# A four-layer graph network on one core: attention sum, norm and last table pass in one stage, weighing on VectorE, and one TensorE signal per four steps

## The chip, the cores and the metric

The kernel runs on one core of one Trainium2 chip. The metric is the device time in microseconds (us). The kernel before took 8360.5 us, the median of three runs (8353.5 to 8371.33).

## What is computed

A graph with 6250 nodes of 256 features and 100000 edges, sorted by target node, goes through four layers. Each is a residual sum followed by a layer norm:

```python
x = _layernorm(x + _L0_gnn_ref(x, src, dst, edge_type_32, edge_weight1, ...))   # 32 relations
x = _layernorm(x + _L1_gnn_ref(x, edge_weight1, ..., src, dst, edge_type_16))   # 16 relations, gated
x = _layernorm(x + _L2_gnn_ref(x, W, a_src, a_dst, edge_W, edge_b, bias, ...))  # attention, 8 heads
x = _layernorm(x + _L3_gnn_ref(x, weight, edge_weight1, src, dst, edge_type_20))# 20 relations
```

Layers 0, 1 and 3 are relational: every node is multiplied with a 256x256 matrix per relation (a table of node x relation rows), each edge takes the row of its source and its relation times its weight, the rows are summed by target, then relu. Layer 2 is attention: for each edge and head a score, a softmax over the edges of one target, and

```python
attn = ex / jnp.maximum(denom[dst], 1e-10)
out = jax.ops.segment_sum(h_src * attn[..., None], dst, num_segments=n)
return out.reshape(n, H * D) + bias
```

## The kernel before

Nodes are held in windows of 128 (NW1 = 49 windows with nodes, NWIN = 50 with one of padding). The edges are cut into 782 tiles of 128; a tile that crosses into another window is visited once per window, so there are STEPS = 830 steps, rounded up to KP = 832. SLOT = 17 steps stand for one window. One **step** sums one tile: a 128x128 matrix of marks (which edge belongs to which row of the window) is the moving or stationary operand of one f32 matmul on TensorE (PE) with the tile's 128 rows, and VectorE (DVE) adds the result in PSUM to the window's rows. The trace shows such an f32 matmul as two records.

The program is a list of stages with a barrier between them (`run`, `PHASES`). In time order: setup and weights; three table passes of layer 0; "fused" (first walk, its norm and the table of layer 1); "gat" (second walk, norm and the attention projections); scores; softmax; "gather_sum"; "norm"; two table passes of layer 3; and "last" (third walk, norm, output).

**A walk** ("fused", "gat", "last") is written out step by step, without a hardware loop. GpSimd (POOL) gathers the rows of step s out of the table with one indirect DMA (L574) into a ring of NR = 16 slots, after waiting for `step_done` of step s - 16. PE's `step` waits for the marks, for the gather of its slot and for the addition that frees its PSUM bank (three banks in "fused", SB1 = 4 in the other two), then multiplies (L1297) and signals `step_done` after each step. DVE, in `fused_steps`, reads the window's number from `win` (L752), waits for `step_done`, makes the mark of step s + 8 (L788), and adds (L806). Between its steps it does parts of the previous window's norm (`row_norm`, L766 to L776, and `normalise_row`).

**The attention sum** ("gather_sum") is a hardware loop. SP loads eight tiles of saved rows at a time (`reload`, L528, 128x8x264 values), ACT copies the softmax numerators into their first eight columns (`exps`, L1226), POOL multiplies eight tiles in one instruction (`weigh`, L596), DVE builds marks (L732) and adds 264 columns (L747), PE multiplies (L1456).

**Norm** (`residual_norm`, L909 to L932) divides, adds the residual and takes mean and variance over all windows at once. **The passes** of layer 3 (`Pass`, 10 relations each) split the weights in a high and a low part, transpose each window, and for each of the 50 windows and 5 PSUM banks run six 128x512 matmuls (L1280); ACT empties each bank (L1129), SP stores it to the table (L387). They are hardware loops too. "fused" does the same for layer 1 inside its walk: eight banks per window (L1321) between the steps.

Quoted from the walk's DVE part, since all turns on its order:

```python
dve.wait_ge(wk.step_done, s + 1)
if s + G < KP:
    mark(s + G)
if s:
    dve.wait_ge(wk.added, s)
a = acc_[:, bass.ds(window, 1), :].squeeze(1)
dve.tensor_tensor(a, a, ps[:, s % banks, 0:D], ALU.add).then_inc(wk.added, 1)
```

## Time and profile before

| | |
|---|---|
| median of 3 runs | 8360.5 us (8353.5 to 8371.33) |
| the profiled execution, its own time | 8366.55 us |
| its span (first to last instruction) | 8364.7 us |
| PE, PE weight loads, DVE, ACT, POOL busy | 68%, 49%, 45%, 20%, 43% |
| granted TensorE clock, mean | 0.802 |
| moved by DMA | 1231.38 MB, 147 GB/s |

Read the shares with care: they are means over stages that have different limits. The page's forty slices show it at once (each digit is the busy share of a slice of 209 us in tenths):

```
PE   5999996888886555555555555555266665999555554
DVE  2111113555554555544444445687776111444444
```

so what a stage costs, and what waits last in it, is read from that stage alone.

### The profile page before, as it was taken

What the parts mean: (1) busy time and instruction counts of PE and PEld (TensorE: products, weight loads), DVE (VectorE), ACT (ScalarE), POOL (GpSimd) and SP (SyncE); (2) the same over time, 40 slices, a digit from 0 to 9 for tenths busy, and PEclk for the clock granted to TensorE, in tenths of its full rate; (3) what the DMA queues carried; (4) which work ended last, traced back from release to release, by engine and by line L of the source; (5) the groups of instructions that cost most, each with busy time, mean ns of one, the idle gap of its engine ahead of it and who ended that gap; (6) DMA issues with size and microseconds to landing.
All of it is one profiled execution on the core that took longest, in us unless ns stands there. A gap on an engine that the chain in (4) does not pass through costs nothing. (4 is left out here: it accounts for less than half of the span.)

```text
span 8364.7 us, 88481 instructions
## 1 busy us (share of the span) xinstructions
PE 5697.3 (68%) x20891; PEld 4066.0 (49%) x20892; DVE 3801.3 (45%) x9956; ACT 1686.8 (20%) x3167; POOL 3568.4 (43%) x3450
## 2 busy tenths in 40 slices
PE   5999996888886555555555555266665999555554
PEld 2878785666665333333333333134443878333333
DVE  2111113555554555544444445687776111444444
ACT  1444442333332000001111111100001444000000
POOL 0000003666665666665555555044341000566665
PEclk8999998999998767676676677577777999766666
DMA  5444444555554333334555556033332444333333
GB/s 163 187 186 186 172 188 158 185 186 187 186 181 145 109 107 108 108 109 145 189 186 189 189 187 199 34 117 122 114 124 105 186 172 186 115 98 95 98 96 94
DMA packets 395622, 1231.38 MB, mean 147 GB/s; under 512 B 101090, under 2 KB 169420, under 8 KB 355141
## 3 DMA queue, kind: packets, MB, share of 16 engines
q1 hardware_dynamic: 234645, 784.90, 25.1%
q0 software_dynamic: 160752, 443.96, 18.5%
q8 instruction: 82, 1.34, 0.1%
q14 instruction: 143, 1.17, 0.0%
HBM read 636.14 MB, written 592.41 MB: 147 GB/s over the span
## 5 line engine op out<-in xcount | busy, mean ns | idle before, releaser
L574 POOL DMA_INDIRECT ring<-table,idx x2496 | 2373.1, 951 | 3409.4 <-DVEq L813 1310.1
L1280 PE MATMUL ps<-W_r,work_r 128*128 128x512 f32 x7800 | 1842.4, 394 | 3.8 <-DVE work_r L716 3.8
L1297 PE MATMUL ps<-ring,W 128*128 128x256 f32 x3328 | 1132.8, 462 | 787.3 <-DVE A L806 420.6
L1280 PEld LDWEIGHTS ps<-W_r,work_r 128*128 128x128 f32 x7800 | 1454.5, 189 | 300.8 <-issue 5.8
L1297 PEld LDWEIGHTS ps<-ring,W 128*128 128x128 f32 x3328 | 676.7, 225 | 1173.0 <-issue 708.7
L788 DVE TENSOR_SCALAR W<-iota,dloc,norm 128x128 f32<-128x128 f32 x1664 | 589.1, 355 | 1166.0 <-PE ps L1297 585.7
L1129 ACT ACTIVATE A<-ps 128x512 f32<-128x512 f32 x1300 | 777.9, 598 | 1090.7 <-PE ps L1280 1090.7
L1297 PE MATMUL ps<-ring,A 128*128 128x256 f32 x1664 | 608.6, 507 | 438.9 <-DVE X L806 338.8
L712 DVE CAST work_r<-ps 128x256 fp32r<-128x256 f32 x250 | 106.0, 424 | 1525.2 <-PE ps L1269 1525.2
L1297 PEld LDWEIGHTS ps<-ring,A 128*128 128x128 f32 x1664 | 379.6, 251 | 643.0 <-issue 319.8
L806 DVE TENSOR_TENSOR X<-X,ps 128x256 f32 x1664 | 686.5, 413 | 8.8 <-PE ps L1297 4.6
L732 DVE TENSOR_SCALAR onehot<-iota,dloc 128x128 f32<-128x128 f32 x840 | 504.1, 601 | 196.6 <-PE ps L1456 145.5
L1321 PE MATMUL ps<-W_r,work_r 128*128 128x512 f32 x1568 | 577.6, 451 | 0.0
L985 DVE TENSOR_TENSOR A<-A,ps 128x528 f32<-128x528 f32 x416 | 286.8, 703 | 627.8 <-remote 522.2
L788 DVE TENSOR_SCALAR A<-iota,dloc,norm 128x128 f32<-128x128 f32 x832 | 296.7, 357 | 569.9 <-remote 287.3
L586 POOL DMA_INDIRECT ring<-gat_table,ix x416 | 406.9, 978 | 300.5 <-DVE ix L1000 164.7
L586 POOL DMA_INDIRECT A<-gat_table,ix x416 | 401.0, 964 | 272.2 <-DVE ix L1000 140.8
L1410 PE MATMUL ps<-W,onehot 128*128 x832 | 336.9, 545 | 239.5 <-DVE A L985 188.8
L1207 ACT ACTIVATE A<-ps 128x528 f32<-128x528 f32 x416 | 252.4, 611 | 1130.8 <-remote 612.3
L1157 ACT ACTIVATE A<-ps,gate 128x256 f32<-128x256 f32 x784 | 320.9, 472 | 642.4 <-PE ps L1321 400.8
L1410 PE MATMUL ps<-W,targets 128*128 x832 | 298.4, 492 | 212.7 <-DVE A L985 128.5
L1456 PE MATMUL ps<-ring,onehot 128*128 128x264 f32 x832 | 306.0, 528 | 188.3 <-DVE A L747 163.7
(230 smaller groups left out, 5403.3 us busy)
## 6 DMA issues: line engine op xcount, KB each, us to landing
table<-A SPq DMA_DIRECT2D x300, 768.0 KB, 3.3
table<-A SPq DMA_DIRECT2D x200, 512.0 KB, 2.6
table<-A SPq DMA_DIRECT2D x98, 1024.0 KB
rows_dram<-ring SPq DMA_DIRECT2D x52, 1056.0 KB
rows_dram<-A SPq DMA_DIRECT2D x52, 1056.0 KB
ring<-rows_dram SPq DMA_DIRECT2D x52, 1056.0 KB, 4.9
W<-rows_dram SPq DMA_DIRECT2D x52, 1056.0 KB, 4.9
ring<-table,idx POOLq DMA_INDIRECT x2496
```

The lines of the kernel that those rows point to most:

```text
L574: pool.indirect_dma_start(out=f_ring[:, s % NR, :], out_offset=None, in_=src, in_offset=bass.IndirectOffsetOnAxis(ap=idx[:, s:s + 1], axis ...
L586: pool.indirect_dma_start(out=place_[:, j, :], out_offset=None, in_=gat_table, in_offset=bass.IndirectOffsetOnAxis(ap=ix[:, h, j:j + 1], a ...
L732: dve.tensor_scalar(onehot[:, j, :], iota[:, :], dloc[:, s], norm[:, s] if weighed else None, ALU.is_equal, ALU.mult if weighed else ALU.b ...
L788: return dve.tensor_scalar(marks_[:, k % G, :], iota[:, :], dloc[:, k:k + 1], norm[:, k:k + 1], ALU.is_equal, ALU.mult).then_inc(wk.onehot ...
L806: dve.tensor_tensor(a, a, ps[:, s % banks, 0:D], ALU.add).then_inc(wk.added, 1)
L1129: act.activation(dst, ps[:, b, :], ACT.Copy).then_inc(q_bank_free, 1)
L1157: ins = act.activation(f_unit[v][:, (b % 4) * 512 + i * D:(b % 4) * 512 + (i + 1) * D], bank[:, i * D:(i + 1) * D], ACT.Copy, scale=gate[: ...
L1280: ins = pe.matmul(ps[:, b, :], rows[:, u, c, :], w[:, c, b * 512:(b + 1) * 512], start=(n == 0), stop=(n == len(terms) - 1))
L1297: pe.matmul(ps[:, s % banks, 0:D], marks_[:, s % G, :], f_ring[:, s % NR, :], start=True, stop=True).then_inc(wk.step_done, 1)
L1321: ins = pe.matmul(ps[:, SB + 1 + b % 4, :], rows[:, q % 2, c, :], w[:, c, b * 512:(b + 1) * 512], start=(n == 0), stop=(n == len(terms) - 1))
L1410: ins = pe.matmul(ps[:, 4 + 2 * e + k, 0:HROW], targets[h % 2][:, j, :], hbuf[:, bass.ds(regs[j], 1), :].squeeze(1), start=True, stop=True)
L1456: pe.matmul(ps[:, j, 0:GROW], onehot[:, j, :], sum_rows[h][:, j, :], start=True, stop=True).then_inc(b_done, 1)
```

## The change

Stages "gather_sum", "norm" and the two passes of layer 3 are replaced by one stage, "sum", written out step by step like "fused". Per window: 17 steps of the attention sum, in between them the norm of the window before (`residual`, `row_norm`, `normalise_row`), its transpose, and ten banks of six matmuls for the window before that. Rows are loaded four tiles at a time into four places (`s_rows`), the numerators come from a copy in DRAM (`ex_dram`, written at the end of softmax), DVE does the weighing (one instruction per four tiles) and makes four marks with one instruction. There are three PSUM banks for steps, one for the transpose, four for the table. The normed rows go to DRAM (`x3_dram`) and are read back in the last stage. In the second walk and the last stage PE signals `step_done` once per four steps, and takes PSUM space for eight steps (two groups of four, two steps to a bank). All walks do 830 steps instead of 832. In softmax the clearing of the sums moves from DVE to POOL.

```diff
+            def finished(self, s):
+
+                return s // self.group + 1
+
+            def place(self, s):
+
+                slot = s % (self.spaces * self.group)
+                bank, half = (slot // 2, slot % 2) if self.group > 1 else (slot, 0)
+                return ps[:, bank, half * D:(half + 1) * D]
...
-        walk0 = Walk("s0", 0, R0, 0, p0[0].table)
-        walk1 = Walk("s1", NRR, R1, 1, table1.rearrange("n c -> (n c)"))
-        walk3 = Walk("s3", 2 * NRR, R3, 2, p3[0].table)
+        walk0 = Walk("s0", 0, R0, 0, p0[0].table, GROUP0)
+        walk1 = Walk("s1", 1, R1, 1, table1.rearrange("n c -> (n c)"), GROUP1)
+        walk3 = Walk("s3", 2, R3, 2, table3.rearrange("n c -> (n c)"), GROUP1)
...
-                   ("gather_sum", None), ("norm", 2)] + relational(p3, walk3)[:-1] + [("last", walk3)])
+                   ("sum", None), ("last", walk3)])
...
+            def keep_ex(_):
+                sp.wait_ge(m_out, QM // BLK + 1)
+                load(ex_dram, W[:, NSC:2 * NSC])
                 sp.wait_ge(loaded, seen[0])
...
+                def load_rows(c):
+                    if c >= 4:
+                        sp.wait_ge(s_done, CH * (c - 3))
+                        sp.wait_ge(s_exp, c - 3)
+                        sp.wait_ge(s_weighed, c - 3)
+                    sp.dma_start(s_ex[:, c % 4], ex_dram[:, c * CH * HEADS:(c + 1) * CH * HEADS].rearrange("p (k h) -> p k h", h=HEADS)
+                                 ).then_inc(s_ex_in[c % 4], 16)
+                    half = c % 2 * CH * GROW
+                    sp.dma_start(s_rows[c % 4], rows_dram[c // 2, :, half:half + CH * GROW].rearrange("p (s c) -> p s c", c=GROW)
+                                 ).then_inc(s_row[c % 4], 16)
...
+                for k in range(NW1 + 2):
+                    p, q = k - 1, k - 2
+                    for j in range(SLOT):
+                        s = k * SLOT + j
+                        c = s // CH + 3
+                        if s % CH == 0 and 7 <= c < CHUNKS:
+                            load_rows(c)
+                        if j == 10 and 0 <= p < NW1:
+                            g = 2 * NW1 + p
+                            sp.wait_ge(f_normed, g + 1)
+                            sp.dma_start(x3_rows[bass.ds(at[p], 1)].squeeze(0), f_xs[:, g % 2, :]).then_inc(f_x_out[g % 2], 16)
+                            if p + 2 < NW1:
+                                load_x(p + 2)
+                        if j == 11 and q >= 0:
+                            store_unit(q, 0)
+                        if j == 2 and q >= 1:
+                            store_unit(q - 1, 1)
+                store_unit(NW1 - 1, 1)
...
-                for s in range(KP):
+                for s in range(STEPS):
                     if s >= NR:
-                        pool.wait_ge(wk.step_done, s - NR + 1)
+                        pool.wait_ge(wk.step_done, wk.finished(s - NR))
...
+            def clear(_):
+
+                pool.memset(XF[:, 0:NW1 * GROW], 0.0)
...
-                            dve.wait_ge(wk.step_done, s + 1)
-                            if s + G < KP:
+                            dve.wait_ge(wk.step_done, wk.finished(s))
+                            if s + G < STEPS:
                                 mark(s + G)
                             if s:
                                 dve.wait_ge(wk.added, s)
                             a = acc_[:, bass.ds(window, 1), :].squeeze(1)
-                            dve.tensor_tensor(a, a, ps[:, s % banks, 0:D], ALU.add).then_inc(wk.added, 1)
+                            dve.tensor_tensor(a, a, wk.place(s), ALU.add).then_inc(wk.added, 1)
...
+            def attention_sum(_):
+                def weigh(c):
+                    rows_ = s_rows[c % 4][:, :, HEADS:GROW].rearrange("p k (h d) -> p k h d", d=HD)
+                    dve.wait_ge(s_row[c % 4], 16 * (c // 4 + 1))
+                    dve.wait_ge(s_ex_in[c % 4], 16 * (c // 4 + 1))
+                    dve.tensor_tensor(rows_, rows_, s_ex[:, c % 4].unsqueeze(3).to_broadcast([P, CH, HEADS, HD]), ALU.mult).then_inc(s_weighed, 1)
+
+                def mark(c):
+                    dve.tensor_tensor(s_marks[:, c % 2 * CH:(c % 2 + 1) * CH, :], iota[:, :].unsqueeze(1).to_broadcast([P, CH, P]),
+                                      dloc[:, c * CH:(c + 1) * CH].unsqueeze(2).to_broadcast([P, CH, P]), ALU.is_equal).then_inc(s_marked, 1)
...
+                for k in range(NW1 + 1):
+                    p = k - 1
+                    for j in range(SLOT):
+                        s = k * SLOT + j
+                        if s < STEPS:
+                            c = s // CH
+                            if s + 1 < STEPS:
+                                window_next = register_of(win, s + 1, NW1 - 1)
+                            dve.wait_ge(s_done, s + 1)
+                            if s:
+                                dve.wait_ge(s_added, s)
+                            a = s_acc[:, bass.ds(window, 1), :].squeeze(1)
+                            dve.tensor_tensor(a, a, ps[:, s % SB, 0:GROW], ALU.add).then_inc(s_added, 1)
+                            window = window_next
+                            if s % CH == 1 and c + 2 < CHUNKS:
+                                weigh(c + 2)
+                            if s % CH == CH - 1 and c + 2 < CHUNKS:
+                                mark(c + 2)
+                        if k == 0 and 4 <= j < 4 + S_BANKS:
+                            low(j - 4)
+                        if k >= 1:
+                            residual(p, j)
+                            row_norm(None, 2, p, j - 2, None)
+                            if j == 9:
+                                normalise_row(2 * NW1 + p)
+                            if j == 14:
+                                xt_high_part(p)
+                            if j == 15:
+                                xt_low_part(p)
...
+            def sum_copies(_):
+                def exps(c):
+                    act.wait_ge(s_row[c % 4], 16 * (c // 4 + 1))
+                    act.wait_ge(s_ex_in[c % 4], 16 * (c // 4 + 1))
+                    act.activation(s_rows[c % 4][:, :, 0:HEADS], s_ex[:, c % 4], ACT.Copy).then_inc(s_exp, 1)
...
+                def evacuate_bank(q, b):
+                    v, n = b // (S_BANKS // 2), b % (S_BANKS // 2)
+                    if n == 0 and q >= 1:
+                        act.wait_ge(s_unit_free[v], 16 * q)
+                    act.wait_ge(s_bank_full, S_BANKS * q + b + 1)
+                    act.activation(s_unit[v][:, n * 512:(n + 1) * 512], ps[:, SB + 1 + (S_BANKS * q + b) % 4, :], ACT.Copy).then_inc(s_bank_free, 1)
...
-            def step(wk, s, marks_, banks):
+            def step(wk, s, marks_):
                 pe.wait_ge(wk.onehot_ready, s + 1)
-                pe.wait_ge(got[s % NR], wk.arrived(s // NR))
-                if s >= banks:
-                    pe.wait_ge(wk.added, s - banks + 1)
-                pe.matmul(ps[:, s % banks, 0:D], marks_[:, s % G, :], f_ring[:, s % NR, :], start=True, stop=True).then_inc(wk.step_done, 1)
+                pe.wait_ge(got[s % NR], wk.arrived(s))
+                if s >= wk.spaces * wk.group and s % wk.group == 0:
+                    pe.wait_ge(wk.added, s - (wk.spaces - 1) * wk.group)
+                ins = pe.matmul(wk.place(s), marks_[:, s % G, :], f_ring[:, s % NR, :], start=True, stop=True)
+                if s % wk.group == wk.group - 1 or s == STEPS - 1:
+                    ins.then_inc(wk.step_done, 1)
...
+            def sum_products(_):
+                def step(s):
+                    c = s // CH
+                    if s % CH == 0:
+                        pe.wait_ge(s_marked, c + 1)
+                        pe.wait_ge(s_weighed, c + 1)
+                        pe.wait_ge(s_exp, c + 1)
+                    if s >= SB:
+                        pe.wait_ge(s_added, s - SB + 1)
+                    pe.matmul(ps[:, s % SB, 0:GROW], s_marks[:, s % (2 * CH), :], s_rows[c % 4][:, s % CH, :], start=True, stop=True).then_inc(s_done, 1)
...
+                for k in range(NW1 + 2):
+                    p, q = k - 1, k - 2
+                    for j in range(SLOT):
+                        s = k * SLOT + j
+                        if s < STEPS:
+                            step(s)
+                        if q >= 0:
+                            if j == 0:
+                                pe.wait_ge(s_xt_ready, q + 1)
+                                pe.wait_ge(s_w_low, S_BANKS)
+                            for b in range(S_BANKS):
+                                if j == BANK_TICKS[b]:
+                                    bank_products(q, b)
+                        if 0 <= p < NW1 and j == 12:
+                            turn_row(p)
```

Not shown: `residual` (in the order below: L1128, L1131, L1137, L1142 of the changed kernel, for maximum, reciprocal, product and residual sum), `low`, `high`, `bank_products` and `turn_row`, which are as in "fused" but with `S_BANKS` = 10 banks; `BANK_TICKS` is 1, 2, 4, 5, 7, 8, 10, 11, 13, 14; GROUP0 = (1, 3), GROUP1 = (4, 2); `s_unit` are two stages of five banks.

DVE in the middle of the attention sum, the kernel before (L732 makes a mark, L747 adds, ISA rows hold waits):

```order
L732 ISA [waits b_done]
L732 TENSOR_SCALAR onehot<-iota,dloc 128x128
L747 ISA [waits b_added]
L747 TENSOR_TENSOR A<-A,ps 128x264
L742 REGISTER_ALU
```

DVE in the middle of the new stage (L1174 adds, L1109 weighs, L1112 makes four marks, L802 reads the window's number):

```order
L1109 TENSOR_TENSOR ring<-ring,work 128x4x256 [waits s_ex_in0,s_row0]
L1131 RECIPROCAL S<-S 128x8 [waits s_ln]
L802 TENSOR_LOAD win
L1174 ISA [waits s_added,s_done]
L1174 TENSOR_TENSOR X<-X,ps 128x264
L1137 ISA [waits f_turned,f_x_out1,s_ln]
L1137 TENSOR_TENSOR onehot<-X,S 128x256
L802 TENSOR_LOAD win
L1174 ISA [waits s_added,s_done]
L1174 TENSOR_TENSOR X<-X,ps 128x264
L1112 TENSOR_TENSOR targets<-iota,dloc 128x512
L1142 TENSOR_TENSOR onehot<-onehot 128x256 [waits f_x_in1,s_ln]
```

The marks have left their place ahead of each addition, and the weighing, with its waits for two loads, and the residual's parts stand between additions.

PE in the middle of the attention sum, the kernel before:

```order
L1447 UNCONDITIONAL_BRANCH [waits bar]
L1447 ISA
L1454 ISA [waits b_mult]
L1456 MATMUL ps<-ring,onehot 128x264 [waits b_added,b_onehot]
L1454 REGISTER_ALU
```

PE in the new stage (L1578 is a step, L1595 a bank):

```order
L1578 MATMUL ps<-ring,targets 128x264 [waits s_added]
L1578 MATMUL ps<-ring,targets 128x264 [waits s_exp,s_added,s_weighed,s_marked]
L1595 MATMUL ps<-W_r,work_r 128x512 [waits s_bank_free]
L1595 MATMUL ps<-W_r,work_r 128x512
L1595 MATMUL ps<-A_r,work_r 128x512 x2
L1595 MATMUL ps<-W_r,work_r 128x512 x2
L1578 MATMUL ps<-ring,targets 128x264 [waits s_added]
L1595 MATMUL ps<-W_r,work_r 128x512 [waits s_bank_free]
L1595 MATMUL ps<-W_r,work_r 128x512
```

A bank's six matmuls now stand between two steps.

PE in the last stage, before and then after:

```order
L1297 MATMUL ps<-ring,W 128x256 [waits s3_added,got8,s3_onehot_ready]
L1297 MATMUL ps<-ring,W 128x256 [waits s3_added,got9,s3_onehot_ready]
L1297 MATMUL ps<-ring,W 128x256 [waits s3_added,got10,s3_onehot_ready]
L1297 MATMUL ps<-ring,W 128x256 [waits s3_added,got11,s3_onehot_ready]
L1297 MATMUL ps<-ring,W 128x256 [waits s3_added,got12,s3_onehot_ready]
```

```order
L1419 MATMUL ps<-ring,W 128x256 [waits got3,s3_onehot_ready]
L1419 MATMUL ps<-ring,W 128x256 [waits s3_added,got4,s3_onehot_ready]
L1419 MATMUL ps<-ring,W 128x256 [waits got5,s3_onehot_ready]
L1419 MATMUL ps<-ring,W 128x256 [waits got6,s3_onehot_ready]
L1419 MATMUL ps<-ring,W 128x256 [waits got7,s3_onehot_ready]
L1419 MATMUL ps<-ring,W 128x256 [waits s3_added,got8,s3_onehot_ready]
```

The wait for the addition stands at every fourth step only.

## Rows read from the trace of the kernel before

**Rows 1.** Busy time by engine in stretches of time, with the granted clock.

```profile
core 0: us, PE busy (x) PEld busy (x) DVE busy (x) ACT busy (x) POOL busy (x), PEclk, DMA share, GB/s
2618.00:3826.00 1208.00, 693.32 (x1966) 442.53 (x1966) 626.38 (x2019) 50.42 (x195) 793.50 (x832) 0.70 0.37 107
7156.00:8364.00 1208.00, 629.85 (x1664) 374.10 (x1664) 593.71 (x1910) 14.41 (x49) 790.30 (x832) 0.68 0.33 96
5417.00:6364.00 947.00, 601.05 (x1664) 383.56 (x1664) 750.23 (x1673) 26.66 (x104) 378.75 (x104) 0.77 0.34 119
6364.00:6424.00 60.00, 0.00 (x0) 0.00 (x0) 56.15 (x68) 6.37 (x7) 0.00 (x0) 0.50 0.14 44
6424.00:7154.00 730.00, 712.41 (x3200) 584.59 (x3200) 124.44 (x356) 304.03 (x505) 0.00 (x0) 0.98 0.45 183
1680.00:1890.00 210.00, 183.03 (x783) 144.47 (x782) 106.48 (x346) 80.68 (x169) 136.63 (x144) 0.96 0.56 186
5449.40:5451.20 1.80, 1.80 (x9) 1.48 (x9) 0.95 (x4) 0.26 (x1) 0.19 (x1) 0.98 0.17 70
```

**Rows 2.** Timeline, attention sum: one pause of VectorE beside GpSimd, then steps.

```profile
start us, us, engine line op out<-in xcount [idle before <-releaser]
...
5701.61 3.64 POOL L596 TENSOR_TENSOR ring<-ring 128x2048 f32<-128x2048 f32 x1 [4.10 <-ACT ring L1226]
...
5704.04 1.28 DVE L732 TENSOR_SCALAR onehot<-iota,dloc 128x128 f32<-128x128 f32 x1 [2.12 <-issue]
...
5706.38 0.43 DVE L747 TENSOR_TENSOR A<-A,ps 128x264 f32 x1
```

**Rows 3.** Groups of instructions of the attention sum, 5417 to 6364 us.

```profile
line engine op names shapes xcount | busy us, mean ns | idle before us <-releasers
L732 DVE TENSOR_SCALAR onehot<-iota,dloc 128x128 f32<-128x128 f32 x840 | 504.1, 601 | 196.6 <-PE ps L1456 145.5 <-issue 50.8 <-DVEq L319 0.3
L747 DVE TENSOR_TENSOR A<-A,ps 128x264 f32 x832 | 354.9, 427 | 0.1
```

**Rows 4.** Timeline, norm between the attention sum and the last pass.

```profile
6367.49 13.49 DVE L912 TENSOR_TENSOR A<-A 128x12800 f32<-128x12800 f32 x1
...
6394.86 18.67 DVE L918 BATCH_NORM_STATS2 work<-X  x50 [0.35 <-DVE X L914]
...
6418.72 5.77 DVE L695 TENSOR_TENSOR W_r<-W,W_r 128x1024 fp32r<-128x1024 f32 x5 [1.25 <-ACT W_r L1114]
```

**Rows 5.** Timeline, last pass at its end and the start of the last stage.

```profile
7150.52 0.60 ACT L1129 ACTIVATE A<-ps 128x512 f32<-128x512 f32 x1 [0.76 <-PE ps L1280]
7154.14 1.02 DVE L882 SCALAR_TENSOR_TENSOR idx<-srcf,types 128x832 int32<-128x832 f32 x1 [16.36 <-SPq L319]
```

**Rows 6.** Timeline, last stage: a slow stretch and the start of the next fast one.

```profile
7502.56 0.40 DVE L788 TENSOR_SCALAR W<-iota,dloc,norm 128x128 f32<-128x128 f32 x1 [3.52 <-remote]
...
7506.76 0.35 DVE L788 TENSOR_SCALAR W<-iota,dloc,norm 128x128 f32<-128x128 f32 x1 [3.52 <-remote]
7506.99 0.94 POOL L574 DMA_INDIRECT ring<-table,idx  x1 [1.58 <-remote]
...
7510.44 0.41 DVE L806 TENSOR_TENSOR A<-A,ps 128x256 f32 x1
...
7511.02 0.41 DVE L806 TENSOR_TENSOR A<-A,ps 128x256 f32 x1
```

**Rows 7.** What GpSimd waited for in the last stage, 7156 to 8364 us.

```profile
POOL ring L574 <- issue: 193.4, 601, 2.7
POOL ring L574 <- remote: 116.4, 69, 3.2
```

**Rows 8.** Timeline, end of the second walk: additions with no mark between.

```profile
3816.31 0.42 DVE L806 TENSOR_TENSOR X<-X,ps 128x256 f32 x1 [0.21 <-DVE X L806]
```

**Rows 9.** Page, part 6: DMA issues, KB of each, median us to landing.

```profile
table<-A SPq DMA_DIRECT2D x300, 768.0 KB, 3.3
```

344 lines of the change are left out of this document (191 added, 153 removed).

## The prediction

> **What bounds the kernel now.** I read first the busy time in stretches, one per stage. The two walks whose signals are to be grouped, second walk and last stage, take 1208 us each with PE busy 693 and 630, DVE 626 and 594, POOL 794 and 790 [rows 1]: nothing is full, 1.45 us go by per step (1208/832). The attention sum takes 947 us, with DVE busy 750, PE 601, POOL 379 at a granted clock of 0.77; norm takes 60 us, in which PE does nothing; the two passes take 730, in which PE is busy 712 and DVE 124 [rows 1]. These three stages, which the change replaces, run from 5417.4 to 7154.1 = **1737 us**, and the reader is to see that they are bound by different engines in turn: DVE, then DVE, then PE.
>
> Then I read who is late in each. In the attention sum a pair of mark and addition costs 601 + 427 ns, 1.03 of the 1.14 us per step [rows 3]. The mean of 601 is no honest price of a mark: alone it is 0.28 to 0.40, but beside POOL's multiplication of eight tiles (3.64 us) DVE stops for 2.12 us and its mark then takes 1.28 [rows 2, 6]. In the passes a bank comes every 1.36 us (0.76 of waiting for PE and 0.60 of copying) to the end, at clock 0.98 [rows 1, 5]: pure PE.
>
> The timeline of the last stage shows two paces. In the fast one additions follow each other every 0.58 us. In the slow one DVE waits 3.52 us for one step, twice running, and PE with it; after some four such steps the fast pace is back [rows 6]. POOL needs 0.95 us per gather (790/832) plus 0.32 between gathers where nothing holds it (193.4/601), so 1.27 per step, and it waits 116.4 us for late signals [rows 1, 7]. So a walk's mean of 1.45 is above POOL's pace, and its slow stretches are the difference. I do not know what makes them.
>
> **The change, part by part.** The sum is made against the profiled execution: 8366.55 us (6 above the median of 8360.5), of which 8364.7 is its span.
>
> *PE in the new stage, per window of 17 steps.* A step leaves two records. In the attention sum 9 of them took 1.80 us at clock 0.98, so 0.40 a step; over the whole stage it is 601/832 = 0.72 at clock 0.77, 0.56 at full clock, waits in between among it [rows 1]. I take 0.44, near the first, which is undisturbed. So 17 x 0.44 = 7.5, ten banks x 1.36 [rows 5] = 13.6, one transpose some 0.4: **21.4 us**.
>
> *DVE, per window.* Additions 17 x 0.43 = 7.3 [rows 2, 3]. Weighing: 4.25 instructions of 1024 elements; a 1024-element product takes 5.77/5 = 1.15 [rows 4], so 4.9. Marks: 4.25 of 512 elements; 13.49 us for 12800 elements is 1.054 ns each [rows 4], and 256 elements take 0.41 [rows 6], so 0.14 are fixed, and 512 cost 0.68: 2.9. (Ends: 0.54 by elements alone, and 4 x 0.28 = 1.12; between them 2.5 us per window.) The norm's parts: some nine instructions of up to 256 elements at up to 0.42, 3.8, statistics 18.67/50 = 0.37 among them [rows 4]. Where two additions stand together 0.21 lies between them [rows 8]; some six such gaps, 1.3. Sum **20 us**. What the weighing costs DVE it had paid already, in pauses beside POOL; POOL now does nothing here, and ACT's ten banks x 0.60 and two stores lie beside PE.
>
> *DMA, per window.* Rows in 2.30 MB, table out 2.62, numerators and x rows some 0.33: 5.25 MB. At 768 KB in 3.3 us with nothing overlapped [rows 9] that is 22 us; transfers do overlap, so it stays hidden, but with little to spare. If the cover went, the window would be 22, not 21.4. SP's queue: a load of rows waits for the step that frees its place; the store issued behind it waits with it. A load is issued 12 steps ahead of its use, some 17 us, which is longer than both.
>
> *How the two meet.* Neither 21.4 nor 20 will be reached, since PE waits for an addition three steps back and DVE for a step. The nearest row is the first walk, built alike: 210 us hold 144 gathers at clock 0.96 [rows 1], 1.46 per step, 24.8 us per 17 steps with eight banks. Its PE work by the prices above is 7.5 + 10.9 + 0.4 = 18.8, so it loses 6.0, of which POOL's pace (17 x 1.27 = 21.6) explains half. The new stage has no gathers. I take half of the loss, 2.6: **T = 24 us**. Ends: 21.4 and 27.5 (24.8 and two more banks).
>
> *The stage.* Start 6 us; window 0 alone with the load and split of ten weight banks 35 (the splits alone 10 x 1.25 + 10 x 1.15 = 24, [rows 4]); window 1 without banks 20; 47 x 24 = 1128; two windows of tail, banks only, 30; last store and barrier 5. Sum 1224, against 1737: **-513**. What goes is norm's 60 us, now between steps, and the passes' PE work lies beside DVE's additions.
>
> *Two steps fewer per walk*, three walks: 3 x 2 x 1.45 = **-9**. *Softmax:* a clearing goes from DVE to POOL and a write of 3.4 MB is added; at 3.3 us for 768 KB it is at most 15 us, and a clearing of the same size as the sums (13200 elements, by 1.054 ns at most 14) leaves: **0**.
>
> *One signal per four steps.* It removes 622 signals per walk. PE needs one wait for an addition in four, from four to eight steps back. DVE may begin adding only when the fourth step is done; its additions then have 0.42 + 0.21 between starts [rows 8] or a mark between, so the fast pace stays 0.58 to 0.63. POOL's slot comes free up to three steps later. In the trace the pause is not at the count of waits but in the arrival: DVE, PE and POOL all see a step late at once [rows 6]. Bounds: a gain down to POOL's pace, and a loss of three steps of ring. I take **0**, since the fast pace is DVE's and the slow one has no cause in sight that a number of signals would change. The Trainium skill (TensorE: Matmul & The Clock Gate, The cost: per-tile semaphore tail) says that completion signals serialise at some 26 ns each; by it 622 fewer would give an estimated 16 us per walk, 33 in both, and 7812 in place of my time. No row here shows it: the fast steps are paced by the additions.
>
> Sum: 8366.55 - 513 - 9 = **7845 us**. A window of 21.4 takes 122 off, one of 27 adds 141: 7720 to 7980 for this case alone.
>
> **Rivals.** *A: late signals are a matter of signals.* Slow stretches appear where PE signals every step to three engines while POOL gathers, and not in the passes, where it signals once per bank [rows 5, 6]. If a signal in four ends them, both walks fall to POOL's 1.27 per step, 830 x 1.27 = 1054 and some 15 for start and end, against 1208: -140 each. 7845 - 280 = **7565**. Against it: the attention sum signals each step too and shows pauses only beside POOL's multiplications [rows 2].
>
> *B: the new stage runs like the first walk*, or at the attention sum's clock of 0.77 [rows 1]: 21.4/0.77 = 27.8, much like 27.5 from the first walk. 47 x 3.5 = +165: **8010**. For it: PE still waits for DVE at each step, as where the clock was 0.77. Against it: ten banks leave PE little idle, and with eight the clock was 0.96. The Trainium skill (TensorE: Matmul & The Clock Gate, HAM oscillation) has it that idle gaps which come back in each round of a loop throw TensorE to its lower clock each time; by it the stage would be this rival. The trace agrees for the attention sum alone.
>
> *C: the ring releases late.* A group's slots come free only with its last step, so POOL is held up to three more steps per group when it is the pace: that would double what a walk now loses against POOL's pace, 1.45 - 1.27 = 0.18 per step, 150 per walk, 300 in both: **8145**. Against it: sixteen slots less three are still 16 us of gathers (13 x 1.27).
>
> *D, the other side: slower.* The slow stretches belong to programs written out step by step, whatever they gather. Then the new stage's steps take 1.45 each as the walks' do, with banks on top: 17 x 1.43 + 13.6 = 37.9 per window (1.43 is 1208 less some 20 for start and end, over 832), and the stage is 96 + 47 x 37.9 = 1877, 140 above 1737: 7845 + 653 = **8498**. It decides from (1737 - 96)/47 = 34.9 us per window on. For it: all three written-out walks have a step of 1.45, the looped sum 1.14 [rows 1]. Against it: the first walk carries eight banks within its 1.46, which such a sum would put at 2.1.
>
> That the change doesn't do what it says is no case: the order of instructions shows banks between steps and one wait in four.
>
> **How the numbers follow.** Forecast 0.48, A 0.30, B 0.14, C 0.05, D 0.03. The range reaches down to take in A with half of its spread (7500) and up over B (8030); it leaves out C, D and the fast window under A, some 0.15. In the forecast's own case it is 7720 to 7980. About 0.2% is what a measurement of this kernel can tell from no change, 17 us. Only D is above 8366; a stage near 35 us per window would give no change. So faster 0.96, same 0.01, slower 0.03.
>
> **What would show it.** In the changed kernel's profile: 17 additions of L1174 each 23 to 25 us; the granted clock there above 0.9; L1109 at 1.15 and L1112 at 0.68; ACT's banks one after another with gaps of 0.76; no DVE mark over 0.5 us in that stage. Last stage and second walk still 1200 us, with the same pauses of 3.5 us, now at a group's first step; if they take 1070, A is right; if POOL's waits for PE grow by over 100 us, C. If the clock in the new stage is 0.8, or a window takes 27 us or more, B. I am wrong in the main if T is over 30: then PE and DVE wait for each other in a way that the first walk did not show.

## The result and the profile after

The changed kernel takes 7772.5 us (median of 4 runs, 7767.9 to 7779.15) against 8357.3 of the kernel before (4 runs): a ratio of 0.930, 95% interval 0.928 to 0.931. The forecast was 7845, its range 7500 to 8030. Its profiled execution took 7774.4 us, span 7772.7, so 592 us less than the one that the prediction was made against.

Where they went shows best stage by stage, from the first instruction of one stage to that of the next on the timeline (softmax from the last gather of the scores; the new stage from its first marks, L1112, to the index product of the last stage, L930):

| us | before | after | difference | forecast |
|---|---|---|---|---|
| to the first walk | 1339.4 | 1337.9 | -1.5 | 0 |
| first walk | 1276.9 | 1276.8 | -0.1 | -3 |
| second walk and scores | 2574.9 | 2577.6 | +2.7 | -3 |
| softmax | 226.2 | 222.1 | -4.1 | 0 |
| attention sum, norm, two passes | 1736.7 | 1150.0 | **-586.7** | -513 |
| last stage | 1210.6 | 1208.3 | -2.3 | -3 |

The stages can be told apart in the forty slices of the kernel before, whose row of PE reads in full (the section on the time before prints three digits 5 too many):

```profile
PE   5999996888886555555555555266665999555554
```

Busy time in stretches of the changed kernel, as [rows 1] had it of the kernel before: second walk, last stage, the new stage, first walk.

```profile
core 0: us, PE busy (x) PEld busy (x) DVE busy (x) ACT busy (x) POOL busy (x), PEclk, DMA share, GB/s
2615.00:3826.00 1211.00, 631.74 (x1956) 467.46 (x1956) 615.22 (x2014) 50.63 (x190) 791.35 (x830) 0.76 0.37 107
6564.00:7772.00 1208.00, 524.27 (x1660) 388.56 (x1660) 582.20 (x1907) 14.42 (x49) 787.84 (x830) 0.73 0.35 101
5414.00:6564.00 1150.00, 1089.84 (x4698) 873.42 (x4698) 820.18 (x1746) 345.98 (x758) 0.00 (x0) 0.98 0.68 229
1339.00:2615.00 1276.00, 1050.26 (x4502) 820.54 (x4502) 640.62 (x2013) 475.94 (x988) 787.14 (x830) 0.95 0.54 180
```

The new stage has PE busy 1090 of 1150 us at clock 0.98, where the attention sum had 601 of 947 at 0.77 and norm nothing. The two walks whose signals were grouped last as long as before, though their PE is busy less (524 in place of 630 in the last stage) and their clock higher.

The groups of instructions of 1000 us in the middle of the new stage; they answer to [rows 3, 5]. The columns are as there, counts before the bar.

```profile
line engine op names shapes xcount | busy us, mean ns | idle before us <-releasers
L1595 PE MATMUL ps<-W_r,work_r 128*128 128x512 f32 x1778 | 642.8, 442 | 0.0
L1578 PE MATMUL ps<-ring,targets 128*128 128x264 f32 x1508 | 428.1, 389 | 24.1 <-DVE work_r L1155 21.8 <-DVE X L1174 0.7
...
L1174 DVE TENSOR_TENSOR X<-X,ps 128x264 f32 x756 | 321.8, 426 | 261.1 <-PE ps L1578 218.1 <-issue 19.3 <-DVE X L1174 16.9
...
L1109 DVE TENSOR_TENSOR ring<-ring,work 128x1024 f32<-128x1024 f32 x189 | 230.3, 1218 | 0.8 <-DMA ring<-rows_dram 0.6
...
L1330 ACT ACTIVATE A<-ps 128x512 f32<-128x512 f32 x225 | 134.4, 598 | 334.4 <-PE ps L1595 334.4
...
L1112 DVE TENSOR_TENSOR targets<-iota,dloc 128x512 f32<-128x512 f32 x188 | 128.7, 684 | 0.0
```

756 additions in 1000 us are 1.323 us per step, **22.5 us per window** of 17. PE is idle for 24.1 us in all (21.8 of them before a step that waits for the transposed rows' last part, L1155), 0.5 per window; VectorE waits 218 us for PE, and ACT 334 us for banks in this row and 313 in that of its other buffer: all wait for PE. Marks and weighing have their fixed prices, 684 ns per 512 elements and 1218 per 1024; the 601 ns of [rows 3] and its pauses are gone with POOL's multiplication.

VectorE in the timeline near the end of the new stage shows how norm disappeared: L1142 (residual), L818 (statistics) and weighing stand between additions. VectorE still waits 218 us in 1000 for PE, so there was room for them.

```profile
start us, us, engine line op out<-in xcount [idle before <-releaser]
...
6516.80 0.68 DVE L1112 TENSOR_TENSOR targets<-iota,dloc 128x512 f32<-128x512 f32 x1
...
6517.40 0.42 DVE L1142 TENSOR_TENSOR onehot<-onehot 128x256 f32<-128x256 f32 x1
...
6517.74 0.42 DVE L1174 TENSOR_TENSOR X<-X,ps 128x264 f32 x1
...
6518.08 0.42 DVE L818 BATCH_NORM_STATS2 row<-onehot 128x6 f32<-128x256 f32 x1
...
6518.41 0.41 DVE L1174 TENSOR_TENSOR X<-X,ps 128x264 f32 x1
...
6518.74 1.22 DVE L1109 TENSOR_TENSOR ring<-ring,work 128x1024 f32<-128x1024 f32 x1
```

The softmax line is a trade that came out level or a little better: 4.1 us is not far from what the other unchanged lines differ by. The timeline of its end: the last numerators are copied, SP writes them to DRAM, and the new stage's first marks begin only when they have landed.

```profile
5404.14 0.89 DVE L1099 COPY W<-ps 128x128 f32 x4 [2.32 <-PE ps L1566]
5405.11 0.33 SPq L354 DMA_DIRECT2D ex_dram<-W  x1
5414.43 0.69 DVE L1112 TENSOR_TENSOR targets<-iota,dloc 128x512 f32<-128x512 f32 x1 [9.40 <-SPq L342]
```

These 9.3 us are exposed (9.4 by VectorE's own row); what went in return is the clearing of the sums, 11.1 us of VectorE (L1090 of the kernel before), which POOL now does in 10.9 while softmax begins.

### The profile page after: what moved, and what is told of

It is laid out like the page before. It is cut to its first block and busy times, and to the rows that moved or that the text cites. A ratio compares the mean times of both kernels' runs of the same rounds, so it can differ in the third digit from the quotient of the medians.

```text
span 7772.7 us, 84351 instructions
## 1 busy us (share of the span) xinstructions
PE 5295.5 (68%) x20713; PEld 4007.5 (52%) x20714; DVE 3656.2 (47%) x9593; ACT 1694.0 (22%) x3309; POOL 3190.7 (41%) x3341
## 5 line engine op out<-in xcount | busy, mean ns | idle before, releaser
L1419 PE MATMUL ps<-ring,W 128*128 128x256 f32 x3320 | 1023.3, 441 | 896.8 <-DVE A L854 507.2
L1402 PEld LDWEIGHTS ps<-W_r,work_r 128*128 128x128 f32 x4800 | 895.0, 189 | 184.8 <-issue 3.3
L1419 PE MATMUL ps<-ring,A 128*128 128x256 f32 x1660 | 533.9, 485 | 248.0 <-DVE X L854 210.9
L1595 PE MATMUL ps<-W_r,work_r 128*128 128x512 f32 x1960 | 701.1, 440 | 0.0
L1226 ACT ACTIVATE A<-ps 128x512 f32<-128x512 f32 x800 | 478.6, 598 | 669.1 <-PE ps L1402 669.1
L1419 PEld LDWEIGHTS ps<-ring,A 128*128 128x128 f32 x1660 | 406.9, 253 | 361.2 <-issue 213.7
L1534 PE MATMUL ps<-W,onehot 128*128 x832 | 359.9, 576 | 286.6 <-DVE A L998 218.5
L1578 PE MATMUL ps<-ring,targets 128*128 128x264 f32 x1660 | 482.0, 396 | 65.2 <-DVE work_r L1155 23.9
L789 DVE CAST work_r<-ps 128x256 fp32r<-128x256 f32 x150 | 63.6, 424 | 953.8 <-PE ps L1391 953.8
L1174 DVE TENSOR_TENSOR X<-X,ps 128x264 f32 x830 | 353.1, 425 | 278.6 <-PE ps L1578 232.7
```

The costliest lines, as they stand in the source:

```text
L1174: dve.tensor_tensor(a, a, ps[:, s % SB, 0:GROW], ALU.add).then_inc(s_added, 1)
L1226: act.activation(dst, ps[:, b, :], ACT.Copy).then_inc(q_bank_free, 1)
L1402: ins = pe.matmul(ps[:, b, :], rows[:, u, c, :], w[:, c, b * 512:(b + 1) * 512], start=(n == 0), stop=(n == len(terms) - 1))
L1419: ins = pe.matmul(wk.place(s), marks_[:, s % G, :], f_ring[:, s % NR, :], start=True, stop=True)
L1534: ins = pe.matmul(ps[:, 4 + 2 * e + k, 0:HROW], targets[h % 2][:, j, :], hbuf[:, bass.ds(regs[j], 1), :].squeeze(1), start=True, stop=True)
L1578: pe.matmul(ps[:, s % SB, 0:GROW], s_marks[:, s % (2 * CH), :], s_rows[c % 4][:, s % CH, :], start=True, stop=True).then_inc(s_done, 1)
```

## The experiments

**A circumstance that the numbers need.** The runs below were made on three occasions. On the first and third the kernel *before* took 7566 and 7562 us (the third time a single run), on the second 8424; the pair above had 8357. Every comparison here is within one occasion, or says that it is not. That the same program differs by 860 us is a finding of its own, though nobody set it up, and is read at the end of this section.

### signal_each, signal_each_again and after_again: one signal per step or per four

```diff
-        GROUP0, GROUP1 = (1, 3), (4, 2)
+        GROUP0, GROUP1 = (1, 3), (1, 4)
```

Expected of signal_each:

> The changed kernel, with PE again signalling after each step in the second walk and the last stage (four single spaces in PSUM). Theory G (grouping is worth nothing): 7773 +- 16 us, both stages within 5 us of 1207 and 1206. Rival S (each signal costs time on PE, some 26 ns by the Trainium skill, TensorE: Matmul & The Clock Gate, The cost: per-tile semaphore tail): 7790 to 7810. Rival L (grouping holds back additions and ring slots and so ate a gain): below 7750. The pauses of VectorE should come back as single ones of 2.5 to 4 us instead of one of 11 us.

It took 6978.5 us (4 runs), the kernel before 7566.2 (13 runs) on that occasion: ratio 0.922 (0.921 to 0.924). None of the times written down applied, since those were worked out for walks at 1.45 us per step, so the two were run side by side again.

> The changed kernel, unaltered, beside signal_each on one chip. In the runs of signal_each and before_grouped the kernel before took 7566 us, not 8357: their walks had no late completions and went at POOL's pace, 1.25 us per step. If the chip of this run is like that, the kernel before takes some 7566 and this one 6978 (theory G: grouping worth nothing) to 6995 (rival L: it costs what before_grouped showed, 0.23%). If its walks are at 1.45 per step as in the predicted pair, 8357 and 7773.

> The changed kernel with a signal after each step, beside after_again on the same chip. Theory G: within 0.1% of after_again. Rival L: 0.1 to 0.3% faster than after_again, 5 to 20 us. Rival S: slower than after_again by 20 us or more.

Measured, with the kernel before at 8424.0 (9 runs): after_again 7836.6 us, ratio 0.9297 (0.9284 to 0.9310); signal_each_again 7831.8, ratio 0.9298 (0.9285 to 0.9311), 5 runs each. No difference that can be told, and none of the 33 us of rival S. The last stage took 1218.3 and 1220.6 us, the new stage 1150.1 in both.

What grouping changed is the shape of the pauses. What VectorE's marks waited for in the last stage, first with a signal per step, then with one per four (us in total, times, longest):

```profile
DVE W L836 <- remote: 380.9, 113, 4.9
...
DVE W L836 <- PE ps L1419: 135.7, 90, 2.9
...
DVE W L836 <- issue: 82.5, 56, 4.3
```

```profile
DVE W L836 <- remote: 509.5, 62, 11.1
...
DVE W L836 <- PE ps L1419: 63.3, 47, 4.7
...
DVE W L836 <- issue: 35.9, 51, 1.9
```

Nearly twice as many pauses of less than half the length, and the other releasers make up the rest: before its marks VectorE was idle 381 + 136 + 83 = 599 us with a signal per step, 510 + 63 + 36 = 609 with one per four. So the lost time does not go with the number of signals: four products that signal once are late by what four that signal each were.

### before_grouped: the grouping alone in the kernel before

```diff
+            def finished(self, s):
+                return s // 4 + 1 if self.grouped() else s + 1
...
+                if wk.grouped():
+                    if s >= 8 and s % 4 == 0:
+                        pe.wait_ge(wk.added, s - 4)
...
+                if s % 4 == 3 or not wk.grouped():
+                    ins.then_inc(wk.step_done, 1)
```

> The kernel before with the grouping alone (second walk and last stage: one signal per four steps, eight half-bank spaces), everything else as it was, 832 steps each. Theory G: 8357 +- 16 us, PE busy less than 630 us in the last stage by the record, since pauses are gathered into fewer, and a granted clock above 0.68 there. Rival S: 8320 to 8340. If it is 8357, the whole difference of 585 us belongs to the new stage, to 12 us near.

7583.6 us (10 runs) against 7566.2 (13): ratio 1.0023 (1.0011 to 1.0035). Grouping is worth nothing there either; it is 0.2% slower, 17 us, which is small but clear of the interval. Rival S is refuted in sign. The three stages that the change replaces take 1717.6 us in this run (4777.7 to 6495.3), and the new stage 1149.3 in signal_each: -568, to set beside 7566.2 - 6978.5 = 588 in all. So nearly the whole gain is the new stage's on this occasion too. No trace of the kernel before exists from it; against before_grouped's, second walk and scores are 14 us shorter in signal_each and the last stage 7.

### pool_weighs: the weighing of the new stage on GpSimd

```diff
-                    weigh(c)
...
-                            if s % CH == 1 and c + 2 < CHUNKS:
-                                weigh(c + 2)
...
+            def weigh_all(_):
+                for c in range(CHUNKS):
...
+                    pool.tensor_tensor(rows_, rows_, s_ex[:, c % 4].unsqueeze(3).to_broadcast([P, CH, HEADS, HD]), ALU.mult).then_inc(s_weighed, 1)
```

> The changed kernel with the weighing of the new stage on POOL, four tiles per instruction, instead of on DVE. Theory P (the new stage is bound by PE, 98% busy at clock 1.0): the stage stays at 1150 us, the total within 10 us of after_again, although DVE loses 208 x 1.22 = 254 us of work. Rival V (VectorE bounds it): the stage falls by up to 4.9 us per window, 230 us. Rival H (POOL's multiplication holds VectorE back, as in the old loop, where a pause of 2.1 us and a stretched mark stood beside each of 3.64 us): 208 x some 1.8 us of pauses, of which VectorE's slack takes up part; the stage is 50 to 150 us longer.

7827.7 us (4 runs), ratio 0.9293 (0.9278 to 0.9307), beside 0.9297 of after_again. The new stage took 1139.0 us (5467.4 to 6606.4) against 1150.1: 11 less, where the other executions with six products per bank lie between 1149.3 and 1153.0. Busy time in 800 us of the new stage, and six groups in it (POOL's multiplication, then VectorE's additions, marks, attention product, norm and statistics):

```profile
5600.00:6400.00 800.00, 789.83 (x3452) 639.61 (x3451) 538.87 (x1124) 246.48 (x549) 296.94 (x153) 1.00 0.70 237
```

```profile
L682 POOL TENSOR_TENSOR ring<-ring,work 128x1024 f32<-128x1024 f32 x153 | 298.1, 1948 | 504.2 <-DMA ring<-rows_dram 503.9
...
L1180 DVE TENSOR_TENSOR X<-X,ps 128x264 f32 x611 | 259.2, 424 | 250.1 <-PE ps L1582 210.3 <-issue 19.6 <-DVE X L1180 13.8
...
L1119 DVE TENSOR_TENSOR targets<-iota,dloc 128x512 f32<-128x512 f32 x153 | 158.7, 1037 | 0.0
L1144 DVE TENSOR_TENSOR onehot<-X,S 128x256 f32<-128x256 f32 x36 | 37.8, 1049 | 0.0
L838 DVE TENSOR_SCALAR onehot<-onehot,moments 128x256 f32<-128x256 f32 x36 | 37.6, 1043 | 0.0
...
L825 DVE BATCH_NORM_STATS2 row<-onehot 128x6 f32<-128x256 f32 x36 | 15.0, 416 | 0.0
```

611 additions in 800 us: 22.3 us per window in place of 22.5. VectorE is busy 539 us in place of 587 (the same stretch of the changed kernel) and waits for PE 210 us in place of 173: theory P, to 1%. Rival H's mechanism is there all the same. A mark takes 1037 ns on the average and up to 2448, where it took 684; apart from POOL's multiplications its mean is 683 (76 marks), beside them 1387 (77). Additions (which read PSUM) keep 424 and statistics 416. But VectorE had slack for it, and PE is idle even less than before (10.2 us in these 800, where it was 24.1 in 1000). So weighing on VectorE is no part of the gain in this stage: it costs some 11 us there. In the old loop the same stretching made 279 ns (the median of L732) into a mean of 601 [rows 3]: 715 marks apart from POOL's multiplications took 279, 125 beside them 2442. That this set the old loop's pace is argued from VectorE's 750 busy us of 947; no run changes it alone.

### two_terms: PE's work in the banks cut to a third

```diff
-                    terms = [(xt_high, s_high, c) for c in range(2)] + [(xt_high, s_low, c) for c in range(2)] + [(xt_low, s_high, c) for c in range(2)]
+                    terms = [(xt_high, s_high, c) for c in range(2)]
```

> The changed kernel with two instead of six products per bank in the new stage (the low parts of the table's weights and rows are left out), which takes 4 x 0.227 x 10 = 9.1 us of PE work per window away. Theory P: with 13.3 us of PE work left the stage is then set by VectorE, some 17 to 20 us per window, so 150 to 250 us less. If the stage falls by less than 50 us, PE was not its bound but the handshake was.

7704.3 us (one run) against 7836.6, and the new stage 1017.6 in place of 1150.1: -132, a little less than the 150 to 250 of theory P and far above the 50 of the other. The same stretch as above, VectorE's additions in it, and what was waited for:

```profile
5600.00:6400.00 800.00, 626.99 (x2234) 417.56 (x2233) 653.14 (x1420) 268.80 (x609) 0.00 (x0) 0.93 0.77 263
```

```profile
L1174 DVE TENSOR_TENSOR X<-X,ps 128x264 f32 x680 | 287.9, 423 | 110.9 <-PE ps L1578 45.0 <-issue 32.3 <-DVE X L1174 24.4
```

```profile
ACT ring L1318 <- DMA ring<-rows_dram: 227.5, 89, 7.4
...
PE ps L1578 <- DVE X L1174: 102.2, 150, 4.4
```

680 additions in 800 us are 20.0 us per window. Of 9.1 us that PE was spared, 2.5 are gained. PE was the bound, and the next one is close behind: VectorE at 82% (653/800), and now SP's loads of rows come too late (227 us of ACT's waits, up to 7.4 at a time) at 263 GB/s. Which of the two it is, no run separates. The prediction's two estimates for these, 20 and 22 us per window, both lie within 10% of it; as a floor for the transfers 22 was too high, since they were done in 20.0.

### last_no_gathers, last_wait_no_read, loose_gathers, ring8: what holds the walks

Parts of the edits follow; the first three runs change the last stage alone. last_no_gathers leaves out its gathers and PE's waits for them; last_wait_no_read keeps both and multiplies a fixed tile, `XF[:, 0:D]`; loose_gathers gathers, but PE neither waits nor reads, and POOL waits only for the earlier gather in the same slot. The sums are then of other rows than they should be, the instructions as many. ring8 halves the ring in all three walks.

```diff
-                for s in range(STEPS):
+                for s in range(STEPS if wk is not walk3 else 0):
...
-                pe.wait_ge(got[s % NR], wk.arrived(s))
+                if wk is not walk3:
+                    pe.wait_ge(got[s % NR], wk.arrived(s))
```

```diff
-                ins = pe.matmul(wk.place(s), marks_[:, s % G, :], f_ring[:, s % NR, :], start=True, stop=True)
+                ins = pe.matmul(wk.place(s), marks_[:, s % G, :], f_ring[:, s % NR, :] if wk is not walk3 else XF[:, 0:D], start=True, stop=True)
```

```diff
-                    if s >= NR:
+                    if s >= NR and wk is walk3:
+                        pool.wait_ge(got[s % NR], wk.arrived(s - NR))
+                    if s >= NR and wk is not walk3:
```

```diff
-        NR = U
+        NR = 8
```

> The changed kernel, whose last stage issues no gathers and waits for none (its sums are then of whatever lies in the ring): the additions, marks and products are the same. If the late completions of PE come from the gathers (waiting for them, or running beside them), the last stage takes 830 x 0.62 + some 20 = 535 us, the total 7100, and no pause of VectorE is over 1.5 us. If they belong to the written-out handshake of PE and VectorE, or to PE's clock, the stage stays near 1206 and the total near 7773.

> The changed kernel, whose last stage gathers and waits as before but whose products read a fixed tile in place of the gathered rows (sums are of that tile). If a step is late because its gather's arrival is (the wait), the stage stays at 1206 and the total at 7773. If it is late because PE reads SBUF beside the writes of the gathers, the stage falls to POOL's pace, 830 x 1.25 + 20 = 1060, total 7625.

> last_no_gathers again (no gathers in the last stage, the rest as it is). Where the kernel before takes about 8400 us: 638 us for the last stage as on the other occasion and 7836 - 568 = 7268 in all, if PE's late completions need gathers beside them; 1206 and 7836, or anything over 750 for the stage, if they belong to the exchange between PE and VectorE. Where it takes 7566, 6565 as before.

> last_wait_no_read again (gathers and their waits stay in the last stage, the products read a fixed tile). Where the kernel before takes about 8400 us (walks with late completions): if the gathered rows' being read is what delays a product, the last stage falls from 1206 to 1060 us, the total from 7836 to 7690; if not, it stays at 7836. Where it takes 7566, 6990 as before.

> The changed kernel whose last stage still gathers every tile, but PE neither waits for a gather nor reads what it brought, and POOL waits only for the gather before in the same slot, not for PE (the sums are of a fixed tile). Gathers and the exchange between PE and VectorE then run side by side and wait for nothing of each other. Where the kernel before takes about 8400 us: if gathers beside them delay PE's completions, the additions still come in two paces with pauses over 2.5 us while POOL issues; if it is the waiting for gathers, the additions come every 0.62 to 0.76 us and are done after some 640 us, and POOL goes on alone at 1.25 us per gather to 1040. Where it takes 7566: the latter.

> The changed kernel with 8 places for gathered rows in the three walks instead of 16. Where the kernel before takes about 8400 us, the pauses came once in 16 steps (23.3 us), as often as the ring turns. If the pause belongs to the ring's turn, it comes every 8 steps and the walks are 5 to 50% longer, total over 7950; if it comes by time or by steps whatever the ring, the period stays and the total is within 50 us of 7836. Where it takes 7566, POOL sets the pace with either ring: 6985 to 7050.

All of them ran only on the occasions where the kernel before takes about 7565 us, one run each, the first two twice there (as no_gathers_b and wait_no_read_b), so they tell what bounds the walks *there*, and not what makes completions late elsewhere. Last stage and total: last_no_gathers 639 and 6565.4 us (again 641 and 6557.2), last_wait_no_read 1067 and 6992.6 (again 1063 and 6981.4), loose_gathers 1048 and 6962.3, ring8 1079 and 7012.0; signal_each, which is whole, 1062 and 6978.5. The last stage of last_no_gathers, then of loose_gathers in two stretches:

```profile
5925.00:6563.00 638.00, 409.32 (x1660) 299.56 (x1660) 575.51 (x1907) 14.42 (x49) 0.00 (x0) 0.97 0.08 21
```

```profile
5915.00:6560.00 645.00, 414.83 (x1660) 304.81 (x1660) 575.75 (x1906) 14.43 (x49) 488.83 (x513) 0.97 0.43 123
6560.00:6960.00 400.00, 0.00 (x0) 0.00 (x0) 0.00 (x0) 0.00 (x0) 299.68 (x317) 0.50 0.37 106
```

Without gathers all 1660 records of PE and all additions fit in 638 us, 0.77 per step with VectorE busy 576, 90%: VectorE is the nearest to a bound then, and the time is above the 535 written down, which had left out its norm. With gathers beside, that wait for PE in nothing and are waited for by nothing, the same work takes 645 us while POOL issues 513 gathers; POOL then goes on alone. So gathers beside hardly slow the exchange on this occasion, and the whole walk is POOL's: in signal_each 829 gathers from 5912 to 6952 us are 1.25 each. A timeline of signal_each's last stage there, step after step at POOL's beat:

```profile
6512.38 0.35 DVE L836 TENSOR_SCALAR W<-iota,dloc,norm 128x128 f32<-128x128 f32 x1 [0.43 <-PE ps L1419]
6512.62 0.95 POOL L661 DMA_INDIRECT ring<-table,idx  x1 [0.30 <-PE ps L1419]
...
6512.96 0.67 PE L1419 MATMUL ps<-ring,W 128*128 128x256 f32 x2 [0.62 <-DVE W L836]
6513.67 0.35 DVE L836 TENSOR_SCALAR W<-iota,dloc,norm 128x128 f32<-128x128 f32 x1 [0.61 <-PE ps L1419]
6513.87 0.96 POOL L661 DMA_INDIRECT ring<-table,idx  x1 [0.30 <-PE ps L1419]
```

A ring half as large costs some 15 us in the last stage (1079 against 1063 of wait_no_read_b, grouped too, single runs). So the places that rival C of the prediction has a group hold back matter little on this occasion, as before_grouped's 17 us say too.

### The two occasions beside each other

The same stages of the same or nearly the same program, in us: "late" is the pair of this document and after_again, "prompt" before_grouped and signal_each.

| | late: before, after, after_again | prompt: before_grouped, signal_each |
|---|---|---|
| to the first walk | 1339, 1338, 1339 | 1339, 1340 |
| first walk | 1277, 1277, 1294 | 1099, 1098 |
| second walk and scores | 2575, 2578, 2613 | 2129, 2115 |
| softmax, from the last gather of the scores | 226, 222, 222 | 211, 208 |
| attention sum, norm, passes | 1737, -, - | 1718, - |
| the new stage | -, 1150, 1150 | -, 1149 |
| last stage | 1211, 1208, 1218 | 1069, 1062 |

Every line with gathers differs by 13 to 24%. The hardware loop of the scores is among them: from its first gather to its last it takes 1356 us in the changed kernel and 1060 in signal_each, 28% more. Of the stages without gathers none differs by over 1.1%, once softmax is counted from its own start: the 14 us in its line lie before POOL's clearing, in the scores' end, and from there to the new stage the changed kernel and signal_each both take 200.1 us. In the late case the changed kernel's last stage looks like this (of POOL's seven gathers between 7199 and 7207 only the last is shown):

```profile
7196.66 1.97 PE L1419 MATMUL ps<-ring,W 128*128 128x256 f32 x8 [0.96 <-DVE A L854]
...
7199.02 0.41 DVE L854 TENSOR_TENSOR A<-A,ps 128x256 f32 x1
...
7199.58 1.97 PE L1419 MATMUL ps<-ring,W 128*128 128x256 f32 x8 [0.95 <-DVE A L854]
...
7206.77 0.95 POOL L661 DMA_INDIRECT ring<-table,idx  x1 [0.30 <-issue]
7210.59 0.35 DVE L836 TENSOR_SCALAR W<-iota,dloc,norm 128x128 f32<-128x128 f32 x1 [11.16 <-remote]
7210.83 0.95 POOL L661 DMA_INDIRECT ring<-table,idx  x1 [3.11 <-remote]
...
7213.19 5.86 PE L1419 MATMUL ps<-ring,W 128*128 128x256 f32 x16 [11.64 <-DVE A L854]
```

PE's records have a group of four products at 7196.66 and one at 7199.58, 1.97 us each, and nothing after. VectorE and POOL see the first at 7210.59 and 7210.83, some 12 us after its recorded end, and then eight additions run through. [Rows 6] show the same as two single waits of 3.52 us. The trace's events of PE's own signals for the two groups stand at 7210.57 and 7210.66, so it is the signals that come late, or PE's records that stand early.

Late rows are not the cause, as far as the transfers' records tell. The gathers for the first of these groups were issued from 7188.0 to 7191.8. In the last stage the data packets of a gather end 2.4 us after its issue on the median in both kinds of occasion, and at most 4.0 us after it in the changed kernel and in signal_each. Two more facts of the traces bear on it. The pauses over 5 us, 50 in this stage, come every 22.8 us on the median, which is 16 steps, one turn of the ring. And the late traces hold only some 7000 of the 39840 semaphore increments that 2490 gathers make (16 each), 7209 in the changed kernel's, the prompt ones nearly all, 39810 in signal_each's. Whether increments are then delivered late too, or only recorded badly, nothing here shows.

## Why the prediction was right, point by point

- **The new stage, the bulk: right in mechanism, 74 us off in size.** Forecast 1224, measured 1150. The term mis-sized is T: 24 us was PE's 21.4 plus half of what the first walk loses; measured 22.5. PE's prices were near: in pool_weighs, as below, a bank and a step take 1.83 us from one bank's start to the next, where I had 1.36 + 0.44. So PE's work is 22.0 in place of 21.4, and the loss in waiting 0.5, not 2.6. The first walk was the wrong pattern: its loss was POOL's pace and late completions, neither of which the new stage has. It took 1277 us here and 1098 on a prompt occasion (signal_each), where its gathers follow each other every 1.28 us. 47 x 1.5 = 71 of the 74. That PE is the bound is shown by two_terms (PE spared, stage 132 us shorter) and pool_weighs (254 us of VectorE's work taken away, stage 11 us shorter).

```profile
5701.86 0.82 PE L1599 MATMUL ps<-W_r,work_r 128*128 128x512 f32 x2
...
5703.44 0.61 PE L1582 MATMUL ps<-ring,targets 128*128 128x264 f32 x2
...
5703.69 0.82 PE L1599 MATMUL ps<-W_r,work_r 128*128 128x512 f32 x2
```

- **VectorE at 20 us a window:** 1.218 and 0.684 us in place of 1.15 and 0.68; busy 587/800, that is 16.5 us, since instructions that follow each other overlap (after an addition of 0.42 the next starts 0.34 us from its start), which the sum of durations overlooked; two_terms, in which PE no longer sets the pace, takes 20.0.
- **The clock,** which rival B put at 0.77: 0.98 over the stage and 1.00 in its middle. So the case of which the Trainium skill speaks (TensorE: Matmul & The Clock Gate, HAM oscillation), idle gaps in each round of a loop, did not arise: PE is idle for 24 us in 1000 of this stage. B and D are refuted; D's point was 34.9 us per window, and the steps written out take 22.5 with ten banks.
- **Grouping at 0: right, shown three ways** (signal_each_again against after_again, before_grouped, and the last stage's 1208 against 1211). The Trainium skill's 26 ns per signal (TensorE: Matmul & The Clock Gate, The cost: per-tile semaphore tail) would have given 33 us; no run shows them, and before_grouped went 0.2% the other way. On the prompt occasions the walk waits for POOL, so PE's signals could give nothing; on the late ones the reason given, that a number of signals would not change the slow pace, held, while the cause of that pace stayed unknown.
- **Rival A: refuted as put, but its number exists.** Walks at POOL's pace were what it offered for fewer signals, 1054 + 15 us; they do occur, 1062 us in signal_each with a signal after each step and 1069 in before_grouped with one in four. The occasion brings them, not the number of signals.
- **Two steps fewer per walk at -9:** not seen; the walks moved by -0.1, +2.7 (with the scores) and -2.3. The padding steps gather and multiply like the others, but the difference is below what two executions differ by.
- **Softmax at 0:** -4. The write is exposed for 9.3 us, inside the bound of 15.
- **Signs that did not come as written:** 17 additions take 22.5 us, just under the 23 to 25; the pauses of the walks are not the same 3.5 us but fewer and longer, up to 11.1.

**Open:** what makes PE's completions late in stages with gathers on some occasions. The number of signals is excluded (after_again, signal_each_again), and so is the change. Whether a late occasion needs PE to wait for gathers, to read their rows, or only to run beside them was to be told by wait_no_read_b, no_gathers_b and loose_gathers, which met a prompt occasion. So did ring8, which was to tell whether the pauses belong to the ring's turn of 16 steps; that stays open too. The record has chip 7 for the occasion of 7566 us and for that of 8424, chip 5 for that of 7562, so the chip's number alone does not tell them apart. No stage without gathers shows it, which points to gathers but does not show how.

## What to carry to other kernels

When stages in a row are bound by different engines, merge them step by step and price the merged one by the busiest engine's work per unit: here 22.0 us of PE's instructions became 22.5 us of time. Take the allowance for waiting from a stage with the same partners, not from one that merely looks alike; the first walk's loss belonged to gathers. An engine's signals or work are worth removing only if someone waits for that engine: 622 signals per walk were worth nothing, and 254 us of weighing on VectorE were worth 11.

## What was not expected of the hardware

The kernel before took 8357, 8424, 7566 and 7562 us on four occasions, the last a single run, the others within 0.4% of themselves. The difference is nearly all in stages with indirect gathers: a step of the last stage took 1.46 or 1.28 us (1211/830 and 1062/830). The difference between the two kernels stayed (585, 587 and, with a signal per step, 588 us), since the walks are common to both, and the ratio went from 0.930 to 0.922 (that one with a signal per step). So a time measured on one occasion says nothing against one from another.

GpSimd's product of 128x1024 values took 1.95 us where VectorE's took 1.22. Beside it some of VectorE's instructions from SBUF to SBUF were held up: marks took 1.04 us on the mean in place of 0.68, the attention product 1.05 in place of 0.42, the last step of norm 1.04 in place of 0.41. Those that read PSUM (additions, 0.42) and the statistics (0.42) were not.

VectorE's instructions overlap in the records: after an addition of 0.42 us the next began 0.34 us from its start, so VectorE's work of a window, 18.5 us by the sum of durations in the 1000 us above, keeps it busy for 16.5.
